# GNN kernel: the layernorm pass moved into the preparation block, x taken by whole partitions of 391 nodes

## What is computed

```python
h = jnp.maximum(_layernorm(x, axis=-1), 0.0)
x = x + _L0_gnn_ref(h, node_type_3, edge_index, edge_type_4, ...)   # typed attention over the edges
h = jnp.maximum(_layernorm(x, axis=-1), 0.0)
x = x + _L1_gnn_ref(h, L1_gnn_W1, L1_gnn_b1, L1_gnn_W2, L1_gnn_b2, src, dst)   # two graph convolutions
```

## Time and profile before

| | us |
|---|---|
| median of 3 runs | 2852.71 (2852.1 to 2857.18) |
| profiled execution, its own time | 2854.7 |
| its span in the trace | 2853.0 |
| preparation, histogram part | 30 to 185 |
| preparation, what follows the histogram | 185 to 216 |
| norm pass with its barriers | 216 to 473.6 |
| attention and all after it | 473.6 to 2853 |

### The profile page before, as it was taken

The page is one execution under the profiler, slowest core; times in us unless marked ns, Lnnn a source line. Parts: engine busy times, 40 slices in busy tenths (PEclk is TensorE's granted clock), DMA queues, the critical chain, the costliest instruction groups (busy, mean ns, idle before and its releaser), DMA issues. The chain is left out here.

```text
span 2853.0 us, 48869 instructions
## 1 busy us (share of the span) xinstructions
PE 1866.8 (65%) x12706; PEld 1449.3 (51%) x12706; DVE 2062.4 (72%) x7060; ACT 1159.7 (41%) x3211; POOL 1655.0 (58%) x1737
## 2 busy tenths in 40 slices
PE   4630001999999999999992677887757763333332
PEld 1100000999999999999992344444435442222221
DVE  7994563999999999999996777777745553333333
ACT  0000001777777777777771345554422221111111
POOL 0002334777777777777761354455467767777776
PEclk9985555999999999999996798899855555555555
DMA  2006774777777777776761344444344442222222
GB/s 52 0 0 202 249 247 134 172 185 184 183 183 184 181 184 185 185 181 184 182 171 33 91 127 123 122 118 124 102 122 132 131 118 72 71 71 70 71 70 52
DMA packets 400270, 374.38 MB, mean 131 GB/s; under 512 B 60254, under 2 KB 342269, under 8 KB 397032
## 3 DMA queue, kind: packets, MB, share of 16 engines
q1 hardware_dynamic: 360856, 276.76, 35.3%
q0 software_dynamic: 31360, 64.76, 10.7%
q10 hardware_dynamic: 7806, 29.98, 2.6%
HBM read 227.43 MB, written 147.13 MB: 131 GB/s over the span
## 5 line engine op out<-in xcount | busy, mean ns | idle before, releaser
L1683 DVE TENSOR_TENSOR_SCAN conv_sT<-keep,conv_sT,conv_pT 128x128 f32<-128x128 bf16 x390 | 187.1, 480 | 384.3 <-PE conv_pT L1658 383.5
L1658 PE MATMUL conv_pT<-ident,conv_row 128*128 128x128 f32 x392 | 182.1, 464 | 405.2 <-ACT conv_row L1643 328.3
L814 POOL DMA_INDIRECT att_xsd<-xt,ends_i x392 | 390.2, 995 | 95.1 <-issue 94.7
L1658 PEld LDWEIGHTS conv_pT<-ident,conv_row 128*128 128x128 f32 x392 | 74.5, 190 | 496.2 <-ACT conv_row L1643 384.9
L995 PE MATMUL att_kvc<-att_hm,w_kv 128*128 128x128 f32 x2352 | 295.9, 276 | 0.0
L939 ACT ACTIVATE att_nhb<-att_nxr 128x128 f32<-128x128 f32 x391 | 168.8, 478 | 276.6 <-DMA att_nxr<-xt 276.6
L995 PEld LDWEIGHTS att_kvc<-att_hm,w_kv 128*128 128x128 f32 x2352 | 279.6, 193 | 0.0
L1368 POOL TENSOR_TENSOR edge_glm<-edge_gl,edge_mask 128x1536 f32<-128x1536 f32 (+1 forms) x56 | 153.1, 2735 | 214.2 <-PE edge_pc L1459 207.4
L1664 PE MATMUL conv_pm<-w,conv_sT 128*128 128x128 f32 x784 | 258.9, 434 | 12.1 <-DVE conv_res L1690 11.0
L1643 ACT ACTIVATE conv_row<-conv_row,ats 128x128 f32<-128x128 f32 x196 | 78.6, 401 | 425.3 <-DMA conv_row<-t,idx 425.3
L1108 DVE TENSOR_TENSOR att_kvm<-att_kvc,att_rel_in 128x1024 f32<-128x1024 f32 x196 | 240.0, 1224 | 13.1 <-PE att_kvc L1008 1.2
(11 more groups left out here) (240 smaller groups left out, 4883.6 us busy)
## 6 DMA issues: line engine op xcount, KB each, us to landing
att_mask_in_t<-type_row SPq DMA_DIRECT2D x196, 192.0 KB
xt<-xr ACTq DMA_DIRECT2D x23, 1224.0 KB
att_nxr<-xt SPq DMA_DIRECT2D x97, 262.0 KB
att_rel_in<-rel_row SPq DMA_DIRECT2D x196, 128.0 KB, 3.2
out_dram<-att_not SPq DMA_DIRECT2D x97, 256.0 KB, 3.8
ta<-att_nhs SPq DMA_DIRECT2D x97, 256.0 KB
xr<-in_x_dram SPq DMA_DIRECT2D x22, 1088.0 KB
xd_rows<-att_xsd SPq DMA_DIRECT2D x196, 65.5 KB, 3.1
```

Source lines behind the costliest of these rows:

```text
L814: pool.indirect_dma_start(out=xsd[:, v, k, :], out_offset=None, in_=xt, in_offset=bass.IndirectOffsetOnAxis(ap=ends_i[:, n, k:k + 1], axis ...
L1658: nc.tensor.transpose(pT[:, n % 2, 0:P], row[:, n % R], ident[:]).then_inc(t_ready, 1)
L1683: dve.tensor_tensor_scan(sT[:, n % R], keep[:, n * P:(n + 1) * P], pT[:, n % 2, 0:P], before, ALU.mult, ALU.add).then_inc(s_ready, 1)
```

## The change

The block of the norm pass is gone, and its work stands in the preparation's block. The nodes are cut another way: partition p holds nodes 391p to 391p + 390, and group g is columns 17g to 17g + 16 of every partition, so 128 pieces of 17 rows lie 391 rows apart. Partition 127 holds only the last 343 nodes (TAIL), so its part of each load is a transfer of its own, the main one covers 127 partitions, and in groups 20 to 22 (RAGGED is 20) the columns that nothing loads are set to zero on POOL. There are nine buffers `xr`; SP issues nine loads right after the index lists. Types and degree columns are no longer read from HBM but copied on chip, types by POOL, degree columns by ACT; `om` is made once for all nodes by four instructions of DVE; `attr` is not written. DVE finishes group g - 1 after the statistics of group g. Stores still go out on ACT's queue, one per group, 128 partitions.

```diff
+TAIL = N - (P - 1) * LO
+RAGGED = TAIL // NG
+XB = 9
...
 @block.sync
                     sp.dma_start(ty_i[:], type_pad.rearrange("(p l) -> p l", p=P)).then_inc(ty_in, 16)
+
+                    def load(g):
+                        b, l0 = g % XB, g * NG
+                        n = min(max(TAIL - l0, 0), NG)
+                        if g >= XB:
+                            sp.wait_ge(written[b], g // XB * 16)
+                        if n < NG:
+                            sp.wait_ge(pad_set, g - RAGGED + 1)
+                        sp.dma_start(xr[b][0:P - 1, :, 0:D], x[0:(P - 1) * LO].rearrange("(p l) d -> p l d", l=LO)[:, l0:l0 + NG]).then_inc(loaded[b], 16)
+                        if n:
+                            at = (P - 1) * LO + l0
+                            sp.dma_start(xr[b][P - 1:P, 0:n, 0:D], x[at:at + n].rearrange("(p l) d -> p l d", p=1)).then_inc(loaded[b], 16)
+
+                    for g in range(XB):
+                        load(g)
                     sp.wait_ge(flags_ready, 1)
...
-                    sp.wait_ge(deg_ready, 1)
-                    for k in range(3):
-                        sp.dma_start(attr[k].rearrange("(p l) -> p l", p=P), at3[:, k]).then_inc(stored, 16)
-                    sp.wait_ge(stored, 16 * 9)
+                    sp.wait_ge(t1d_set, 1)
+                    sp.dma_start(t1[EP:EP + 1], t1d[:]).then_inc(stored, 16)
+                    for g in range(XB, NGROUPS):
+                        load(g)
+                    sp.wait_ge(stored, 16 * 7)
...
 @block.scalar
+                    act.wait_ge(deg_ready, 1)
+                    def degrees(g):
+                        b = g % XB
+                        if g >= XB:
+                            act.wait_ge(written[b], g // XB * 16)
+                        nc.scalar.activation(xr[b][:, :, C_SO:C_IDX + 1].rearrange("p j k -> p k j"), at3[:, :, g * NG:(g + 1) * NG],
+                                             ACT.Copy).then_inc(so_done, 1)
+                    for g in range(AHEAD):
+                        degrees(g)
+                    for g in range(NGROUPS):
+                        act.wait_ge(so_done, g + 1)
+                        act.wait_ge(type_done, g + 1)
+                        act.wait_ge(row_ready, g + 1)
+                        act.dma_start(xt_g[:, g * NG:(g + 1) * NG], xr[g % XB][:]).then_inc(written[g % XB], 16)
+                        if g + AHEAD < NGROUPS:
+                            degrees(g + AHEAD)
...
 @block.gpsimd
+                    for g in range(AHEAD):
+                        kinds(g)
+                    for g in range(NGROUPS):
+                        pool.wait_ge(var_ready, g + 1)
+                        pool.tensor_tensor(xr[g % XB][:, :, C_RSTD], ve[g % 2][:], mh[:], ALU.pow).then_inc(rstd_ready, 1)
+                        if g + AHEAD < NGROUPS:
+                            kinds(g + AHEAD)
...
 @block.vector
+                    for g in range(NGROUPS):
+                        b = g % XB
+                        parts = sum(2 if h * NG < TAIL else 1 for h in range(b, g + 1, XB))
+                        dve.wait_ge(loaded[b], parts * 16)
+                        if g >= 2:
+                            dve.wait_ge(row_ready, g - 1)
+                        for j in range(NG):
+                            m = dve.bn_stats(st[g % 2][:, j], xr[b][:, j, 0:D])
+                        link(m)
+                        aggregate(st[g % 2], tmp, mv[g % 2][:], ve[g % 2][:], link).then_inc(var_ready, 1)
+                        if g >= 1:
+                            finish(g - 1)
+                    finish(NGROUPS - 1)
...
-            with nc.Block() as block:
-                @block.sync
-                def _(sp):
-
-                    sp.dma_start(t1[EP:EP + 1], t1d[:]).then_inc(stored, 16)
-                    sp.wait_ge(stored, 16 * 10)
-            clear()
```

More of the change, by code:

```diff
@@ L57, with type_cols @@
 assert ET == 2 * HALF and ET == U * EG and NT == NG * NGROUPS and ET == TG * TGROUPS
+def type_cols(rows):
+    return rows[:, :, C_TYPE:C_TYPE + K9]
 def bcast(ap, shape):
@@ L358, in hgt_then_graphconv @@
             tp = [lp(f"tp{i}", [P, 4, HALF], F32) for i in range(2)]
+            xr = [lb(f"xr{b}", [P, NG, RW], F32) for b in range(XB)]
+            st = [lb(f"st{b}", [P, NG, 6], F32) for b in range(2)]
+            mv = [lb(f"mv{b}", [P, NG], F32) for b in range(2)]
+            ve = [lb(f"ve{b}", [P, NG], F32) for b in range(2)]
+            mh = lb("mh", [P, NG], F32)
+            tmp = lb("tmp", [P, 3, NG], F32)
+            om = lb("om", [P, LO], F32)
             hist = [lp(f"hist{i}", [P, LO], F32) for i in range(2)]
@@ L378, in hgt_then_graphconv @@
             ty_in, ty_ready = ls("ty_in"), ls("ty_ready")
+            loaded = [ls(f"loaded{b}") for b in range(XB)]
+            written = [ls(f"written{b}") for b in range(XB)]
+            t1d_set, half_set, pad_set = ls("t1d_set"), ls("half_set"), ls("pad_set")
+            type_done, so_done, var_ready, rstd_ready, row_ready = (
+                ls("type_done"), ls("so_done"), ls("var_ready"), ls("rstd_ready"), ls("row_ready"))
+            AHEAD = XB - 3
+            xt_g = xt.rearrange("(p l) w -> p l w", p=P)
             with nc.Block() as block:
@@ L430, in _ @@
                     nc.scalar.activation(power[:], deg[:], ACT.Sqrt).then_inc(powed, 1)
+                    act.wait_ge(deg_ready, 1)
[14 more added lines that the diff above has]
+                            degrees(g + AHEAD)
+                    for b in range(XB):
+                        act.wait_ge(written[b], 16 * ((NGROUPS - b + XB - 1) // XB))
                 @block.gpsimd
@@ L525, in _ @@
                     link(dve.tensor_scalar_max(t1d[:], b1_all[0:1], 0.0))
+                    dve.sem_inc(t1d_set, 1)
+                    link(dve.tensor_scalar(om[:], ty_hot[:, 0], a3[:, 0:1], None, ALU.mult))
+                    link(dve.scalar_tensor_tensor(om[:], ty_hot[:, 1], a3[:, 1:2], om[:], ALU.mult, ALU.add))
+                    link(dve.scalar_tensor_tensor(om[:], ty_hot[:, 2], a3[:, 2:3], om[:], ALU.mult, ALU.add))
+                    link(dve.tensor_scalar(om[:], om[:], -1.0, 1.0, ALU.mult, ALU.add))
                     link(dve.tensor_scalar(tab_f[:, 0:D], tab_f[:, 0:D], sk9[:], None, ALU.mult))
@@ L602, in hgt_then_graphconv @@
[L602 to L697, removed]
-                        dve.tensor_tensor(am[:], xr[b][:, :, C_TYPE:C_TYPE + K9].rearrange("p j (t k) -> p j t k", k=SPLIT)[:, :, :, 0],
-                                          a3[:].rearrange("p (o t) -> p o t", o=1).to_broadcast([P, NG, TYPES]), ALU.mult).then_inc(stats, 1)
-                        dve.wait_ge(stats, s0 + 6)
-                        dve.reduce_sum(om[:], am[:], AX.X).then_inc(stats, 1)
-                        dve.wait_ge(stats, s0 + 7)
-                        dve.tensor_scalar(om[:], om[:], -1.0, 1.0, ALU.mult, ALU.add).then_inc(stats, 1)
-                        dve.wait_ge(rstd_ready, g + 1)
-                        dve.scalar_tensor_tensor(xr[b][:, :, C_NMR], mv[b][:], -1.0, xr[b][:, :, C_RSTD], ALU.mult,
-                                                 ALU.mult).then_inc(stats, 1)
-                        dve.wait_ge(stats, s0 + 9)
-                        dve.tensor_tensor(xr[b][:, :, C_RA], xr[b][:, :, C_RSTD], om[:], ALU.mult).then_inc(stats, 1)
-                        dve.tensor_tensor(xr[b][:, :, C_NA], xr[b][:, :, C_NMR], om[:], ALU.mult).then_inc(stats, 1)
-                        dve.wait_ge(stats, s0 + 11)
-                        dve.sem_inc(row_ready, 1)
-                    node_groups(dve, norm)
```

35 lines of the change are left out of this document (23 added, 12 removed).

## The result

| | before | changed |
|---|---|---|
| median us | 2854.94 | 3662.06 |
| runs | 4 | 4 (3661.09 to 3666.0) |
| ratio, 95% interval | | 1.2835 (1.2814 to 1.2855) |

The changed kernel is 28.35% slower. One of the four runs of before beside it was disturbed (3608 us) and is left out of the ratio; in all its other runs here the kernel took 2849.91 to 2857.18 us.

The account below looks back on a forecast made before the run. The prediction took loads of x on one DMA engine to bound the norm pass: 19 + 1350 + 69 + 5 + 14 = 1457 us, 983 us later than before, giving 3836 us, range 3450 to 3980.

Parts of the forecast that it names:

- Width: Norm pass loads of x: each load of 127 partitions runs on one DMA engine, bounds 1 and 16.
- Loads as one stream, SP held: Loads of x form one stream, groups every 59 to 62 us; SP held by nine loads until about 545 us.
- Time per row: Loads of x: 27 ns per 512 B row on one engine, 1350 us for 50,000 rows; bounds 23.8 and 28.7 ns.
- rival 2: Loads of x: one engine, but 17-row stretches in one piece, 3466 us, or four or five rows, 3676; 20% together.
- Packets: Loads of x: a partition's 17 rows move as single rows of 512 B, not in larger pieces.
- Stores: Norm pass stores: the engine with the loads has a sixteenth of each, 3.0 us, 23 times, 69 us; bounds 0 and 69.
- Last group: End of the norm pass: from the last group's data to the attention stage, 14 us.
- What is hidden: `om`, type and degree columns and power hidden by the loads; histogram within 3 us, nothing changes from the attention stage on.
- Spread over 16 engines: Rival: loads of x spread over 16 engines after all, stage ends near 359 us, 2738 us; 8%.
- Held queues: Rival: a load that cannot be handed out also holds ACT's queue, 30 to 60 us more, up to 3896 us; 7%.

Follow-up runs that it names:

- experiment 1: Kernel before, its loads of x in groups 0 to 21 cut into 127 partitions and 1, same buffers and bytes: 3842.03 us.
- experiment 3: Changed kernel, first nine loads cut into 61 and 13 partitions on SP's queue and 53 on ACT's, later ones into 112 and 15: 2978.01 us.
- experiment 2: Changed kernel, each load of 127 partitions cut into 112 and 15: 2747.79 us, ratio to before 0.9641; also 124 and 3: 2886.9, 122 and 5: 3062.39.

## Why the prediction was right, step by step

- **In short.** The mechanism was right, one DMA engine and one stream of loads. One term of the sum, the time per row, was too high, and it makes nearly all of the difference.
- **Width.** Right: 127 partitions ran on one DMA engine, by the DMA share of 0.08 beside the histogram and the 22 GB/s, and experiment 1 shows it without the rest of the change. The reading that carried it was the share of 0.32 in the last group. The rule of the Trainium skill in "DMA: Bandwidth & Descriptors", section "Why a DMA increments its semaphore by 16 and not by 1", that a transfer gets the largest count up to 16 that divides its slowest dimensions, held at every count tried (1, 2, 4 and 16 engines). By the same section it is always the lowest-numbered engines, so all single-engine loads share one; no row of before could show that, and experiment 3 agrees with it.
- **Loads as one stream, SP held.** Right: issues 51 to 54.5 us apart from the first on (once 59.9, beside the first stores), SP at the stores of the flags at 502.5 us where I had 545.
- **Time per row.** This term was mis-sized. I chose 27 ns, near the weight loads' 28.7; the stream needs 40 us / 1,697 packets = 23.6 ns, next to the lower of my two bounds, 23.8. 50,000 x (27 - 23.6) = 170 us, and that is nearly all of the 174 us between 3836 and 3662. The reason stands in the row: 7.2% of 16 engines over 40 us is 46.1 us of packets, 27.2 ns each. A packet does last 27 ns, but the next one begins 23.6 ns after it has begun. The share of the profile adds up durations, and durations of packets on one engine overlap: by the trace's packet records of these 40 us, one packet was under way for 85% of the time and two for 15%, never none and never three. I read a duration where I needed a distance. On the five engines the two nearly agree (0.305 to 0.32 against 5/16 = 0.3125), and there I had the distance, 23.8. The lower end of the forecast's own range, 3660, does not come out of the sum either: with 23.8 ns it gives 3836 - 160 = 3676, the figure of rival 2, and the result lies just below it.
- **Packets.** Right: single rows of 512 B. Rival 2 (larger pieces) did not happen. That its 3676 lies 14 us from the result is luck: it took the 23.8 ns of the row with larger pieces, and single rows happen to need about the same.
- **Stores.** 69 us predicted. From load to load it is 51.3 us without a store and 54.1 with one (53.9 to 54.4), 2.8 us against 3.0 worked out; in sum the stream lasted from 19 (as guessed) to 1267.4 us, 1248 us, of which 50,000 x 23.6 = 1180 are rows and 68 the rest, stores and flags together, for which I had 74.
- **Last group.** 14 us predicted, 1282.3 - 1267.9 = 14.4 measured.
- **What is hidden.** Right: preparation, `om`, type and degree columns and the power cost nothing, and the later stages kept their time.
- **Rivals.** Spread over 16 engines: did not happen, but experiment 2 is that case made by hand, and its 2748 us stands against 2738 worked out. Held queues: DVE got its weights in time, and stores went out beside blocked loads; ACT was held only in experiment 3, by loads of its own (179 us of DVE's time).

## What to carry to other kernels

Look at the number of partitions of every large transfer: it should have 16 as a divisor. 127 is prime and leaves one DMA engine, and taking the last, shorter partition out of a load makes it. Write the access pattern out for all 128 if you can, else cut at 112. A profile shows the fault as a DMA share a little above a small multiple of 1/16 (0.08, 0.15 and 0.29 here for one, two and four engines). To price a stream, count packets in a stretch in which the queue is never empty and divide the time by them, and take no packet's duration for it. And before loads are moved ahead under an earlier stage, ask how many of them the pass can use: here six loads in the 28 us ahead of it were worth nearly as much as nine under the histogram.

## What the runs showed of the hardware that was not expected

- On one engine 512 B rows last 27.2 ns and follow each other every 23.6 ns; with a second queue on the same engine every 21.8 ns (100 us / 4,593 packets).
- Single rows of 512 B, beside the histogram and with no store, moved at 22 GB/s on one engine, 44 on two and 71 on four. On sixteen it depended on how the load was cut: 204 to 209 GB/s as 112, 15 and 1 partitions (13 for each engine), 302 as one transfer of 128 (19 for each), at DMA shares of 1.08 to 1.14. Why is not shown.
- A transfer issued behind a single-engine load held the issuing engine for 49 to 59 us (SP), and nine of them held ACT; the other engine's queue went on (a store was issued on ACT's in 0.35 us at 227.7 us, while SP was held).
- With the DMA engines full, 128 partitions in one transfer moved 387 GB/s with its stores and the same bytes as 112, 15 and 1 partitions 342, at the same DMA share of 1.07, with 27.3 and 35.3 ns per packet of x.
